# Local attention layers: output projection ahead of the turning of weights, turning in the array's row halves

## The reference

```python
HEADS, DIM_HEAD, WINDOW = 8, 64, 128
def _layer(x, wqkv, ...):                  # twice
    h = shift_token(x)
    q, k, v = jnp.split(h @ wqkv, 3, axis=-1)       # 8 heads of 64
    q, k = l2norm(q) * qs, l2norm(k) * ksc
    q, k = rotary_xpos(q, k)
    o = local_attention(q, k, v)
    x = x + o @ wo
    h = shift_token(x); h = layernorm(h) * lg + lb
    a, g = jnp.split(h @ w1 + b1, 2, axis=-1)
    return x + (a * gelu(g)) @ w2 + b2
def local_attention(q, k, v):
    # windows of 128 queries; keys of the window before and of the own one, j
    sim = einsum('bhwid,bhwjd->bhwij', bq * 8, bk)
    mask = (i < j) | (i > j + WINDOW) | (j == -1)
    attn = softmax(where(mask, -max, sim)); out = einsum('bhwij,bhwjd->bhwid', attn, bv)
```

## Time and profile before

| what | value |
|---|---|
| median of 3 runs | 2335.92 us (2332.85 to 2339.22) |
| profiled execution | 2333.25 us |
| its span | 2331.4 us |
| PE busy | 2239.6 us, 96% |
| PEld busy | 1316.2 us, 56% |
| DVE busy | 1635.1 us, 70% |
| ACT busy | 1254.6 us, 54% |
| POOL busy | 732.4 us, 31% |
| mean granted TensorE clock | 0.989 of full |

### The profile page before, as it was taken

How to read it: one execution, slowest core, us unless ns; L and a number is a source line. 1 busy time by engine, 2 the same in 40 slices (tenths; PEclk the granted TensorE clock), 3 DMA queues, 4 the chain that set the end, 5 groups by cost and what they waited for, 6 DMA issues and landing times.

```text
span 2331.4 us, 42446 instructions
## 1 busy us (share of the span) xinstructions
PE 2239.6 (96%) x16257; PEld 1316.2 (56%) x16306; DVE 1635.1 (70%) x4252; ACT 1254.6 (54%) x2823; POOL 732.4 (31%) x730
## 2 busy tenths in 40 slices
PE   7999999999998999989899999999999999999998
PEld 3333333334634867756566666666666666666665
DVE  6788888886502746668777677677767777787763
ACT  4666666665222622247666656665665665566640
POOL 3344323321111411144433233333333333333321
PEclk7999999999998999999999999999999999999999
DMA  7454343333397020010000000000001000000001
GB/s 240 151 158 121 117 119 122 112 91 109 157 422 297 2 91 19 28 39 3 5 6 6 5 2 6 6 2 32 15 6 53 6 15 24 19 6 24 22 23 40
DMA packets 68617, 158.44 MB, mean 68 GB/s; under 512 B 6256, under 2 KB 49120, under 8 KB 63936
## 3 DMA queue, kind: packets, MB, share of 16 engines
q1 hardware_dynamic: 65856, 146.55, 17.8%
q0 software_dynamic: 2560, 9.18, 1.7%
HBM read 116.39 MB, written 35.13 MB: 65 GB/s over the span
## 4 chain that ended last, share of the span: by engine, by line
PE 73%; DVE 14%; DMA 4%; ACT 4%; issue 3%; POOL 1%; SPq 0%; another core or an unknown queue 0%; POOLq 0%; DVEq 0%; ACTq 0%
PE banks L2073 10%; PE banks L2051 7%; PE banks L1932 6%; PE banks L1946 5%; PE banks L232 4%; PE banks L274 4%; PE banks L2033 3%; PE banks L245 3%; PE banks L1976 3%; PE banks L1991 3%; DMA arena<-in_e_W 3%; DVE arena L483 2%; PE banks L1455 2%; PE banks L1958 2%; PE banks L300 2%
## 5 line engine op out<-in xcount | busy, mean ns | idle before, releaser
L483 DVE TENSOR_REDUCE arena<-banks 128x1 f32<-128x512 f32 x512 | 322.6, 681 | 61.2 <-PE banks L232 60.4
L395 ACT ACTIVATE arena<-banks 128x512 f32<-128x512 f32 x512 | 280.3, 596 | 136.1 <-PE banks L245 112.4
L2073 PE MATMUL banks<-arena 128*128 128x512 f32 x640 | 293.2, 594 | 1.0 <-DVE arena L2258 1.0
L2155 ACT ACTIVATE arena<-arena 128x256 f32<-128x256 f32 (+1 forms) x512 | 286.5, 562 | 5.0 <-DVE arena L2264 4.5
L2411 POOL TENSOR_TENSOR arena<-arena 128x512 f32<-128x512 f32 x128 | 162.8, 1272 | 379.8 <-DVE arena L2295 379.8
L1932 PE MATMUL banks<-arena 128*128 128x512 f32 x512 | 241.5, 594 | 2.8 <-DVE arena L2295 2.8
L232 PE MATMUL banks<-arena 96*128 96x512 bf16 x512 | 202.9, 400 | 14.6 <-DVE arena L483 8.9
L2407 POOL TENSOR_TENSOR arena<-arena 128x16 f32<-128x16 f32 x64 | 189.4, 2959 | 5.4
L2127 ACT ACTIVATE arena<-arena 128x256 f32<-128x256 f32 (+1 forms) x256 | 102.1, 471 | 162.9 <-DVE arena L2240 162.9
L2073 PEld LDWEIGHTS banks<-arena 128*128 128x128 f32 x640 | 115.5, 190 | 126.7 <-issue 116.5
L245 PE MATMUL banks<-arena 128*128 128x512 bf16 x463 | 174.6, 382 | 3.1 <-ACT arena L395 2.2
(11 more groups left out here) (304 smaller groups left out, 4225.7 us busy)
## 6 DMA issues: line engine op xcount, KB each, us to landing
arena<-in_e_W SPq DMA_DIRECT2D x16, 2048.0 KB, 15.6
arena<-stacks SPq DMA_DIRECT2D x64, 384.0 KB, 4.7
arena<-in_e_Wg SPq DMA_DIRECT2D x8, 2048.0 KB, 17.6
stacks<-arena SPq DMA_DIRECT2D x32, 384.0 KB, 2.5
stacks<-arena SPq DMA_DIRECT2D x32, 256.0 KB, 2.8
arena<-dens POOLq DMA_DIRECT2D x32, 256.0 KB, 4.8
arena<-in_xT SPq DMA_DIRECT2D x8, 512.0 KB, 7.8
stacks<-arena SPq DMA_DIRECT2D x32, 128.0 KB, 2.6
```

Of the source, the lines that this page charges most:

```text
L395: e.activation(ex[:, j], self.psum[:, self.exp_bank1(k)], ACT.Exp).then_inc(s["a_e"], 1)
L483: e.tensor_reduce(split(self.maxima[n % 2][:, 0:16], TILES, UNIT)[:, t, j:j + 1], self.psum[:, k % 3], AX.X, ALU.max, negate=True).then_in ...
L2073: i = e.matmul(bank, weights[:, c], self.hT[:, c], start=c == 0, stop=c == 1)
L2155: k = e.activation(pr[:, h, at:], pr[:, h, at:], ACT.Exp, bias=mx[:, h:h + 1], scale=rn[:, h:h + 1], accum_out=den[:, h:h + 1])
```

## The change

- tensor4: the output projection of d stands right behind MLP part 2, and all turning of c behind it.
- tensor4_weights works by couples of pairs (4 heads). Per pair of heads and half of the queries it turns three blocks of 64 queries by 128 columns (64 keys of one head beside 64 keys of the other): 24 turns with 64 rows and a 64-wide identity per tile, 16 for a first tile, alternating between the array's upper and lower rows and between two banks. It waits for both engines' divisions.
- The divided probabilities are written in the order that this needs to probs[1]; probs[0] alone holds the scores. So the maximum of b waits for c's division, and the division for the turning of the tile before.
- vector4_weights and scalar4_weights copy 384 columns (256 in a first tile), VectorE the first query half, ScalarE the second, both couples one after the other. pT has a second set.
- tensor4_values takes tokens with their halves exchanged for every odd head: 4 products of 256 columns. GpSimd makes this copy (gpsimd4_swap, 4 copies of 128x64 per tile) at the start of its slot.
- tensor4_attend uses quarters for a first tile too; ScalarE's copy and VectorE's add are done for it as well.

```diff
@@ tensor4
             self.tensor4_mlp(e, w, n, 2)
+            if d is not None:
+                self.tensor4_out(e, w, d)
             if c is not None:
                 self.tensor4_weights(e, w, c, 0)
                 self.tensor4_weights(e, w, c, 1)
-            if d is not None:
-                self.tensor4_out(e, w, d)
-            if c is not None:
-                self.tensor4_weights(e, w, c, 2)
-                self.tensor4_weights(e, w, c, 3)
             self.tensor4_mlp(e, w, n, 3)
@@ tensor4_values
-        for c in range(CHUNKS):
-            at = 1 - c + t * P
-            k = e.matmul(self.psum[:, 2], self.xT[:, b, c, at:at + P], self.wqkv4[:, c, 2], start=c == 0, stop=c == 1)
+        w.wait_ge("t_swap", i + 1)
+        out = split(self.psum[:, 2], PAIRS, 2, HD4)
+        for hh in range(2):
+            for c in range(CHUNKS):
+                at = 1 - c + t * P
+                tokens = self.swapped[i % 2][:, c] if hh else self.xT[:, b, c, at:at + P]
+                k = e.matmul(out[:, :, hh], tokens, split(self.wqkv4[:, c, 2], PAIRS, 2, HD4)[:, :, hh], start=c == 0, stop=c == 1, skip_group_check=True)
@@ tensor4_weights
+    def tensor4_weights(self, e, w, i, couple):
+        banks = [self.bank4("w", i, 2 * couple + half) for half in range(2)]
+        w.wait_ge("t_pn", 2 * i + couple + 1)
+        w.wait_ge("t_pna", 2 * i + couple + 1)
+        self.emptied4(w, "w", i, 2 * couple)
+        self.emptied4(w, "w", i, 2 * couple + 1)
+        places = [(0, 0, 1), (1, 1, 2), (2, 2, 3)] if i % TILES else [(3, 1, 0), (2, 2, 1)]
+        for n in range(2):
+            for place in places:
+                last = n == 1 and place == places[-1]
+                for half in range(2):
...
+                    rows, at = slice(64 * half, 64 * half + 64), 512 * (2 * couple + n) + P * source
+                    k = e.transpose(banks[half][:, 192 * n + 64 * to:192 * n + 64 * to + 64], self.probs[1][rows, at:at + P], self.ident[rows, rows])
+                    if last:
+                        k.then_inc(self.s["t_pT"], 1)
@@ vector4
             if c is not None:
                 self.vector4_weights(e, w, c, 0)
+                self.vector4_weights(e, w, c, 1)
             if a is not None:
                 self.vector4_rotate(e, w, a, 0)
...
-            if c is not None:
-                self.vector4_weights(e, w, c, 2)
@@ vector4_weights (scalar4_weights: bank 2 * couple + 1, query half 1)
+        to, bank = self.pT[i % 2][couple][:, :, 0], split(self.bank4("w", i, 2 * couple)[:, 0:384], 2, 192)
+        at = 0 if i % TILES else 64
+        w.wait_ge("t_pT", 4 * i + 2 * couple + 1)
...
+        e.tensor_copy(to[:, :, at:], bank[:, :, at:]).then_inc(self.s["t_pTd"], 1)
@@ gpsimd4
             if n < TILES4:
+                self.gpsimd4_swap(e, w, n)
                 self.gpsimd4_tile(e, w, n)
```

More of the change, by code:

```diff
@@ L1836, in layout4 @@
         self.vn = [r.take(512) for _ in range(4)]
-        self.pT = [split(r.take(512), 2, 2, P) for _ in range(4)]
+        self.pT = [[split(r.take(768), 2, 2, 192) for _ in range(2)] for _ in range(2)]
+        self.swapped = [split(r.take(256), CHUNKS, P) for _ in range(2)]
         self.hn = r.take(1024)
@@ L1978, in tensor4_scores, with probs4 @@
             k.then_inc(self.s["t_sc"], 1)
[L1980 to L1992, removed]
+    def probs4(self, i, h):
+        pair, hh = divmod(h, 2)
+        raw = split(self.probs[0][:, 0:2048], H4, 2, 2, 64)[:, h]
+        view = split(self.probs[1][:, 512 * pair:512 * pair + 512], 2, 4, 64)
+        view = view[:, :, 1:3] if hh else view[:, :, 0::3]
+        return (raw, view) if i % TILES else (raw[:, 1:], view[:, 1:])
@@ L1994, in tensor4_attend @@
     def tensor4_attend(self, e, w, i):
-        first = i % TILES == 0
-        w.wait_ge("t_vn", i + 1)
+        w.wait_ge("t_vn", min(i + 3, TILES4))
         if i:
             w.wait_ge("t_o", i)
-        if not first:
             w.wait_ge("t_x", i)
+        own, ahead = self.vn[i % 4], self.vn[(i - 1) % 4]
         for pair in range(PAIRS):
[L2004 to L2012, removed]
+            w.wait_ge("t_pTd", 2 * i + pair // 2 + 1)
+            w.wait_ge("t_pTa", 2 * i + pair // 2 + 1)
+            pT = self.pT[i % 2][pair // 2][:, pair % 2].rearrange("p a b -> p (a b)")
+            outer, inner = split(pT, 3, 2, 64)[:, 1:3, 0], split(pT, 3, 2, 64)[:, 0:2, 1]
+            for hh in range(2):
+                cols = slice((2 * pair + hh) * HD4, (2 * pair + hh + 1) * HD4)
+                for half in range(2):
+                    rows = slice(64 * half, 64 * half + 64)
+                    near = half == hh
+                    v = own if near or i % TILES == 0 else ahead
+                    k = e.matmul(self.psum[64 * hh:64 * hh + 64, 2 if half else 5, pair * P:(pair + 1) * P], v[rows, cols], outer[rows] if near else inner[rows],
+                                 start=True, stop=i % TILES == 0, skip_group_check=True)
+            if i % TILES == 0:
@@ L2013, in tensor4_attend @@
                 continue
             for hh in range(2):
-                for half, (bank, n) in enumerate(((5, 1), (2, 0))):
+                cols = slice((2 * pair + hh) * HD4, (2 * pair + hh + 1) * HD4)
+                for half in range(2):
                     rows = slice(64 * half, 64 * half + 64)
-                    k = e.matmul(self.psum[64 * hh:64 * hh + 64, bank, pair * P:(pair + 1) * P], self.vn[(i - 1 + n) % 4][rows, heads[hh]], self.pT[pair][rows, hh, n],
-                                 start=True, stop=False, skip_group_check=True)
@@ L2024, in tensor4_attend @@
+                    at = 0 if near else 64
+                    k = e.matmul(self.psum[64 * hh:64 * hh + 64, 2 if half else 5, pair * P + at:pair * P + at + 64], (ahead if near else own)[rows, cols],
+                                 pT[rows, 0:64] if near else pT[rows, 320:384], start=False, stop=True, skip_group_check=True)
         k.then_inc(self.s["t_av"], 1)
@@ L2099, in scalar4 @@
                 self.scalar3_norm(e, w, SEQS - 1)
+            self.scalar4_mlp(e, w, n, 1)
+            if n == 2:
                 self.scalar3_turn(e, w, SEQS - 1, 0)
-            self.scalar4_mlp(e, w, n, 1)
-            if d is not None and d % TILES:
+            if d is not None:
                 w.wait_ge("t_av", d + 1)
@@ L2156, in scalar4_exp, with scalar4_weights @@
         k.then_inc(self.s["t_exp"], 1)
[L2158 to L2164, removed]
+    def scalar4_weights(self, e, w, i, couple):
+        to, bank = self.pT[i % 2][couple][:, :, 1], split(self.bank4("w", i, 2 * couple + 1)[:, 0:384], 2, 192)
+        end = 192 if i % TILES else P
+        w.wait_ge("t_pT", 4 * i + 2 * couple + 2)
+        if i >= 2:
+            w.wait_ge("t_av", i - 1)
+        e.activation(to[:, :, 0:end], bank[:, :, 0:end], ACT.Copy).then_inc(self.s["t_pTa"], 1)
     def scalar4_mlp(self, e, w, slot, part):
@@ L2235, in vector4_divide @@
     def vector4_divide(self, e, w, i):
-        at = 0 if i % TILES else P
-        pr, extra = split(self.probs[i % 2][:, 0:2048], H4, 2 * P), self.probs[i % 2][:, 2048:]
+        extra = self.probs[i % 2][:, 2048:]
         den, rden = extra[:, 8:16], extra[:, 16:24]
@@ L2394, in gpsimd4, with gpsimd4_swap @@
             if n < TILES4:
+                self.gpsimd4_swap(e, w, n)
                 self.gpsimd4_tile(e, w, n)
             self.gpsimd4_mlp(e, w, n)
+    def gpsimd4_swap(self, e, w, n):
+        l, b, t = n // LAYER, n // TILES % SEQS, n % TILES
+        if l:
+            w.wait_ge("m_yTd", b + 1)
+            w.wait_ge("m_yTa", b + 1)
+        else:
+            w.wait_ge("r_xTb", b + 1)
+            w.wait_ge("r_xTa", b + 1)
+        if n >= 2:
+            w.wait_ge("t_v", n - 1)
+        for c in range(CHUNKS):
+            at = 1 - c + t * P
+            e.tensor_copy(self.swapped[n % 2][:, c, 0:64], self.xT[:, b, c, at + 64:at + P])
+            k = e.tensor_copy(self.swapped[n % 2][:, c, 64:P], self.xT[:, b, c, at:at + 64])
+        k.then_inc(self.s["t_swap"], 1)
     def gpsimd4_tile(self, e, w, n):
```

58 lines of the change are left out of this document (28 added, 30 removed).

## The result

The changed kernel takes 2359.59 us (median of 4 runs, 2357.41 to 2368.55) against 2335.7 (4 runs), a ratio of 1.011 with a 95% interval of 1.0091 to 1.013: slower by 1.1%. The forecast was 2358, slower by 0.9%. The profiled execution is 2359.54 us with a span of 2357.7.

What follows compares the result with a forecast made beforehand. TensorE and, in slots A and B, VectorE's chain were taken to bound the kernel. Rounds +12.6 and light slots +9.3 us gave +21.9 on the profiled 2333.25, so 2355.2; with the median 2.7 higher, 2358 us (8 in 10: 2332 to 2384).

Steps and rivals of the forecast that it cites:

- The bottleneck: In the first two of four repeating slots, VectorE's chain binds along with TensorE; the two are level in the second.
- The turning: TensorE's row-half turns follow at 0.065 us per pair: 0.78 us a tile instead of 1.76, first tile 0.52 instead of 0.88.
- rival 1: Pairs of turns are bound by their loads at 0.113 us each: +38 us, 2374 us; chance 0.22.
- Changes of the array's form: TensorE going from full to split rows costs 0.1 us, and the same on the way out; two changes per tile.
- The bank wait: First MLP piece of part 3 waits until VectorE empties its bank: 0.36 us saved per slot, 0.26 lost with a first tile.
- VectorE's late start: In slot A VectorE idles 1.55 us before copying turned weights; the chain brings 1.3 us of lateness into slot B.
- Rounds: Each round of four slots grows by 0.84 us; 15 rounds give +12.6 us.
- Light slots: Six early slots without MLP products (n = 2 to 7) each lose 1.3 plus 0.25 us: 9.3 us.
- The swap's share: GpSimd's copies starting beside VectorE's scale hold it up, 0.25 us in each of the six slots without MLP products.
- The ring's share: In slots without MLP products, projection, copies and rotation wait on each other in a ring: 1.3 us later per slot.
- Rivals 2 and 3: VectorE's lateness absorbed: 2333 us, chance 0.15; TensorE alone decides, no wait exposed: 2296 us, chance 0.13.
- Rival 4: The change doesn't do what it says, as with strided reads doubling the values' products: +100 us; chance 0.03.

Runs made afterwards that it cites:

- e2: Only the new order (output projection ahead of all turning, copies adjacent) put on the kernel before, with its full-array turning: 2369.39 us, ratio 1.0155.
- e3: Changed kernel with VectorE's rotation of the queries moved ahead of its two copies of turned weights: 2330.87 us, ratio 0.999.
- e1: Changed kernel's row-half turning kept, but the old order restored on TensorE, VectorE and ScalarE: 2326.36 us, ratio 0.9971.
- e7: Changed kernel with ScalarE's division moved behind the queries' copy and the squares: 2341.19 us, ratio 1.0024.
- e4: Changed kernel without GpSimd's swap copies and the wait for them, all heads reading unexchanged tokens: 2360.66 us (one run).

## Why the prediction was right, step by step

- **The sum.** Predicted 21.9 us more; the profiles show 23.2 (11.7 in the light slots, 11.1 in slots 8 to 62, 0.4 in the tail) and 3.0 of scatter. The rounds were put 1.5 too high and the light slots 2.4 too low. That the total came so close is in part luck; the signs and the mechanism are not.
- **The bottleneck** was read rightly: TensorE and VectorE's chain level at B. e2 and e3 show it from both sides, by moving nothing but order.
- **The turning.** Predicted 0.065 us a pair, from L990's rounds less the difference of the loads. Measured: (0.96 - 0.227) / 11 = 0.067, with the slower first pair in it. The rule of the Trainium skill ("TensorE: Matmul & The Clock Gate", "LDWEIGHTS (loading the stationary operand)") that rows don't shorten a load holds here: 139 ns for 64 rows, 140 for 128. Its figure of columns / 1.2 ns, by which I estimate 107 ns for 128 columns, does not hold as the interval of a turn: pairs whose loads have 128 columns each follow at 0.067. That was rival 1, and it is out: it wanted 0.113.
- **Changes of the array's form.** Predicted 0.1 in and 0.1 out. Measured in e1: 0.34 for both, entry 0.09 gap and a first pair 0.05 longer, exit 0.10 gap and a first product 0.10 longer. Too small by 0.14, but in the changed kernel the way out lies inside the bank wait, so it cost little.
- **The bank wait.** Predicted 0.36 saved in A and C, 0.26 lost in D. Measured 0.31, 0.31 and 0.26; in A and C the entry, 0.14 and not 0.10, makes most of the difference. In the last five rounds, where slot D has one MLP piece fewer, D loses 0.75 (19.25 against 18.50). In e1, e3 and e7 it loses 0.31 there, in e2 0.72. So 0.44 of it is again VectorE's late chain, which I had taken as absorbed in every D.
- **VectorE's late start.** Predicted the first copy 1.55 us later and the scores of B 1.3 later. Measured from the start of slot A (1493.06 before, 1510.21 after), the copy is 1.58 later (13.74 against 12.16), with 1.49 of idle time ahead of it. The end of the second rotation, which GpSimd's add waits for, is 1.13 later, the first line before and the second after:

```profile
1508.80 0.75 DVE L2295 TENSOR_TENSOR arena<-banks,arena 128x256 f32<-128x256 f32 x2
...
1527.08 0.75 DVE L2306 TENSOR_TENSOR arena<-banks,arena 128x256 f32<-128x256 f32 x2
```

  The scale is 1.13 later, the squared lengths 1.13 and the scores 1.12. So from the rotation on the chain passes its lateness on whole, as predicted. What I had too small is what VectorE gives back before it: 0.45 and not 0.26. The score wait went up by 1.14 (0.16 to 1.30), and A and B together grew 0.77 against 0.94 predicted. Its whole path is shown: e3 fills the idle time and B falls by 1.01, e7 shortens a link further on and B falls by 1.06.
- **Rounds.** Predicted 0.84 x 15 = 12.6, measured 11.1 over slots 8 to 62. There are only 13 whole rounds behind slot 10: 8 grow by 0.71 and the last 5, by D's 0.75, by 1.21; slots 8 to 10 together are 0.52 shorter (C 19.01 against 19.79). One miscount makes up for part of the other.
- **Light slots.** Predicted 9.3, measured 11.7: a size near enough, for partly wrong reasons. The swap's share (1.5) is zero by e4. The ring's share, 7.8, measures 11.7 - 3 x 1.1 = 8.4. The other 3.3 is the clock (last section).
- **Rivals 2 and 3** (absorbed; TensorE alone) are ruled out by the 1.30 us in B. Rival 4 too: the values' four products take 1.99 us after and 1.98 before, so the strided reading costs nothing.

What the runs don't settle: the 11.7 us of the light slots were not taken apart by an experiment of their own. That they are a ring through projection, copies and rotation is read from TensorE's wait of 2.00 us for the rotation (below) and from e3, where the rotation stands ahead and they take 83.1 us in all. The parts agree with it: the order alone adds 9.4 us to them (e2, at a granted clock of 1.00), the turning alone takes 0.7 off (e1), and 8.7 is near the 8.4 above.

## What to carry to other kernels

Before moving a long operation ahead of a short one on the busiest engine, look at who is fed by the short one and whether that engine has anything else to do meanwhile: here 1.7 us of projection bought 1.5 us of idle VectorE, paid a slot later. A round in which one engine is busy 99.8% of the time can still have a second one level with it; the places to look are waits of 0.1 to 0.6 us that recur in every round, those of the weight loads with them. And where one engine's list holds a long operation that nobody needs yet ahead of short ones that the chain does, as ScalarE's division here, the exchange is free and worth as much as the work on the array.

## What the runs showed of the hardware that I had not expected

**The clock fell behind some of the new waits.** In the light slots TensorE now waits twice per slot. Timeline, slot 5 of the changed kernel:

```profile
1083.65 3.68 PE L1926 MATMUL banks<-arena 128*128 128x512 f32 x4 [2.00 <-DVE arena L2306]
...
1087.60 1.88 PE L1926 MATMUL banks<-arena 128*128 128x512 f32 x4
...
1095.00 1.97 PE L2046 MATMUL banks<-arena 128*128 128x256 f32 x8 [0.78 <-ACT arena L2163]
```

The same four products take 3.68 us after a wait of 2.00 and 1.88 half a slot later. Over those 3.68 us the granted clock (the third figure from the end) is 0.54, so the array ran at 1.2 GHz instead of 2.4 for nearly all of them:

```profile
1083.65:1087.33 3.68, 3.68 (x6) 1.54 (x7) 2.30 (x6) 0.89 (x4) 3.34 (x5) 0.54 0.00 0
```

It happened in slots 3, 5 and 6, each time behind the wait for the rotation, and made each of them 1.1 us longer; in slots 4 and 7, with waits as long (1.99 and 1.86), it did not. Before the change none of the six had it. e4 has it in the same three slots, e7 in 3, 5 and 7. In e3, where the wait for the rotation is gone and that of 0.78 us stays, the clock stays at 1.00 there and the six slots take 83.1 us. In e2, where TensorE waits 1.56 to 1.61 us at the same place, it stays at 1.00 too. So in these slots the clock fell only behind the longer waits, and not behind each of them; what decides between them these runs don't show.

**A GpSimd copy beside a VectorE operation can be the one that waits.** The rows of before show VectorE held for as long as a GpSimd operation of 2.35 us lasts, and I had priced the swap from that. Timeline of a light slot after:

```profile
1102.67 0.24 POOL L2422 COPY arena<-arena 128x64 f32<-128x64 f32 x1
1102.77 0.69 DVE L2314 TENSOR_TENSOR arena<-arena 128x512 f32<-128x512 f32 x1 [1.38 <-POOL arena L2439]
1102.85 0.71 POOL L2423 COPY arena<-arena 128x64 f32<-128x64 f32 x1
```

The scale keeps its 0.69 us, and the second copy takes 0.71 instead of 0.24. A wider copy, early in slot B, starts as shortly behind the scale, and there the scale takes 1.21:

```profile
1529.20 1.21 DVE L2314 TENSOR_TENSOR arena<-arena 128x512 f32<-128x512 f32 x1 [0.72 <-POOL arena L2439]
1529.26 0.60 POOL L2459 COPY arena<-arena 128x512 f32<-128x512 f32 x1
```

So the swap's copies of 128x64 left VectorE's operation alone, while a copy of 128x512 (0.60 us) and the operation of 2.35 us ran beside scales of 1.21 and 2.82. What decides who waits is open.
